# A decoder layer in one program: four cross attentions in one stretch between attention and feed-forward, and both pairs of batches through a seven-product feed-forward

## The reference

```python
def reference(x, ctx_1024, ...):            # x (4, 512, 512), ctx (4, 512, 256), float32
    ...
    x = layernorm(x + attention(x))         # 16 heads of 32, RoPE, causal softmax
    # cross attention: the context attends to itself, and its map mixes the columns of x
    query = ctx @ Wq.T + bq                 # (4, 512, 128)
    key = ctx @ Wk.T + bk
    att = softmax(query @ key.T)            # (4, 512, 512)
    x = layernorm(x + einsum('bln,bmn->blm', x, att))
    # feed-forward, hidden size 2048
    x = layernorm(x + (silu(x @ Wg.T) * (x @ Wu.T)) @ Wd.T)
```

## Time and profile before

| | |
|---|---|
| median of 3 runs | 1010.21 us (1010.11 to 1010.47) |
| profiled execution, its own time | 1012.47 us |
| its span, first to last instruction | 1010.6 us |
| granted TensorE clock, mean over the span | 0.990 |
| busy: PE, PEld, DVE, ACT, POOL | 955.7, 773.9, 690.2, 497.2, 466.3 us |
| slot 192 of the scores begins | 299.3 us |
| the first product of the pair steps begins | 755.95 us |

### The profile page before, as it was taken

The page is one execution under the profiler, slowest core; times in us unless marked ns, Lnnn a source line. Parts: engine busy times, 40 slices in busy tenths (PEclk is TensorE's granted clock), DMA queues, the critical chain, the costliest instruction groups (busy, mean ns, idle before and its releaser), DMA issues. The chain is left out here.

```text
span 1010.6 us, 15936 instructions
## 1 busy us (share of the span) xinstructions
PE 955.7 (95%) x5344; PEld 773.9 (77%) x5344; DVE 690.2 (68%) x1474; ACT 497.2 (49%) x1104; POOL 466.3 (46%) x489
## 2 busy tenths in 40 slices
PE   6788999999998889899999999999999999999997
PEld 4556877777777666688888887888887878888885
DVE  5566777778765787655555568555547888777876
ACT  4576777777775674344415433441343333332332
POOL 2466645645864523232123113212566666655644
PEclk9999999999999999899999999999999999999999
DMA  5975666955765652253212303221122121110002
GB/s 217 245 187 156 181 184 158 251 147 145 209 181 135 188 148 84 94 211 112 94 35 91 113 34 157 83 95 59 67 94 69 57 103 55 41 63 32 1 1 83
DMA packets 43040, 117.76 MB, mean 117 GB/s; under 512 B 5200, under 2 KB 5328, under 8 KB 40912
## 3 DMA queue, kind: packets, MB, share of 16 engines
q1 hardware_dynamic: 42960, 116.75, 37.7%
HBM read 91.56 MB, written 25.17 MB: 115 GB/s over the span
## 5 line engine op out<-in xcount | busy, mean ns | idle before, releaser
L961 ACT ACTIVATE prob<-prob,nmax 128x512 f32<-128x512 f32 (+3 forms) x256 | 144.0, 563 | 101.1 <-DVE nmax L1230 99.3
L1230 DVE CUSTOM_DVE_ANT_0 prob<-ps,mask 128x512 f32<-128x512 f32 (+3 forms) x256 | 124.4, 488 | 94.2 <-PE ps L649 88.7
L1672 POOL TENSOR_TENSOR g_lo<-gated,g_hi 128x512 fp32r<-128x512 f32 x32 | 41.3, 1289 | 205.5 <-ACT g_hi L1061 205.5
L649 PE MATMUL ps<-ks,qs 128*128 128x256 f32 (+2 forms) x256 | 105.1, 412 | 7.3 <-DVE nmax L1230 5.6
L1565 POOL TENSOR_TENSOR raw<-raw,cos 128x512 f32<-128x512 f32 x32 | 42.8, 1338 | 91.2 <-DVE pj L1212 64.8
L1351 DVE TENSOR_TENSOR dn_lo<-f_raw,dn_hi 128x512 fp32r<-128x512 f32 x32 | 30.5, 954 | 48.9 <-ACT dn_hi L1047 48.9
L649 PEld LDWEIGHTS ps<-ks,qs 128*128 128x128 f32 x256 | 48.9, 191 | 17.9 <-DVE nmax L1230 8.1
L634 PE MATMUL pj<-xT_hi,w_hi 128*128 128x512 f32 x128 | 52.9, 413 | 9.2 <-ACT xT_hi L931 6.1
L1574 POOL TENSOR_TENSOR raw<-raw,qk_hi 128x512 fp32r<-128x512 f32 x32 | 42.2, 1319 | 30.4 <-ACT qk_hi L955 30.4
L1374 DVE SCALAR_TENSOR_TENSOR half<-th,pg 128x512 f32<-128x512 f32 x32 | 22.0, 686 | 46.5 <-ACT th L1053 46.5
L634 PE MATMUL pj<-xT_hi,w_lo 128*128 128x512 f32 x128 | 51.4, 402 | 1.5 <-DVE w_lo L1187 1.5
(11 more groups left out here) (416 smaller groups left out, 2859.5 us busy)
## 6 DMA issues: line engine op xcount, KB each, us to landing
f_raw<-in_w_ffn SPq DMA_DIRECT2D x48, 768.0 KB, 4.2
qs<-qk_scratch SPq DMA_DIRECT2D x64, 256.0 KB, 4.6
ks<-qk_scratch SPq DMA_DIRECT2D x60, 256.0 KB, 7.4
qk_scratch<-qk_hi SPq DMA_DIRECT2D x32, 256.0 KB, 2.0
qk_scratch<-raw SPq DMA_DIRECT2D x32, 256.0 KB, 2.0
res<-in_x SPq DMA_DIRECT2D x4, 1024.0 KB, 5.8
x_scratch<-res SPq DMA_DIRECT2D x4, 1024.0 KB, 4.7
x_raw<-in_xT SPq DMA_DIRECT2D x12, 256.0 KB, 2.8
```

The source lines that it names most:

```text
L649: pe.matmul(ps[:, t % 2, 0:w], qs[n % 2][:, r, s * P:(s + 1) * P], ks[n % 2][:, r, 0:w], start=True, stop=True).then_inc(s_done, 1)
L961: act.activation(prob[:, t % PROBS, 0:w], prob[:, t % PROBS, 0:w], ACT.Exp, bias=nmax[:, n % 2, i:i + 1], scale=-1.0, accum_out=rsum[:, n ...
L1230: dve.tensor_tensor_reduce(prob[:, t % PROBS, 0:w], ps[:, t % 2, 0:w], mask[:, S - w:S], -D ** -0.5, 3e38, ALU.add, ALU.min, accum_out=nma ...
L1672: pool.tensor_tensor(g_lo[:, i % 2, :], gated[:], g_hi[:, i % 2, :].bitcast(F32), ALU.subtract).then_inc(glo_done, 1)
```

## The change

- All four cross attentions stand ahead of the feed-forward, as units in slots. That of batch 0 begins at slot 224 (table `CROSS`), those of batches 1 to 3 and the last output projections o12 to o15 are laid over one another in 45 further *ticks*, 256 to 300 (table `TICKS`; the number behind the colon is the PSUM bank, of eight). A tick is a slot without scores. Units of even and odd batches have their own sets of SBUF tiles.
- The single-batch feed-forward (`hidden`, `down`, `step`) is gone. Both pairs run through the seven products: NH = 32 pair steps. The 32 steps before had 36 matmuls each, so a pair took 72 for a hidden block; now 66.
- At the turn between the pairs (TURN = 15) the moving operands are renewed: 14 groups of four transposes (`renewed`), each with a cast on ScalarE and a remainder on VectorE, stand behind the products of step 15 and behind p1 of step 16. Step 15 has no parts, step 16 has eight. The sums for the second pair are made on GpSimd in steps 12 to 15 (`next_sums`).
- NR is 2: the load of weight block h waits for the operands of step h - 2 and for its down rows, which are now split in the step that owns them.
- The normalization after the cross attention ends on ScalarE and not on VectorE. The finished rows of batches 0 and 1 are normalized in steps 18 to 20.
- The projections q14 to k15 and o8 to o11 stand at the regular slots of every earlier group.

```diff
-ALONE = 2
-STEPS = ALONE * HT
-NR = 4
+PAIRS = B // 2
+NH = PAIRS * HT
+NR = 2
...
-BEGIN, END = -29, SCORES + 24
+BEGIN, END = -29, SCORES + 48
...
+CROSS = [(("c", 0), 224, (6,), 0), (("c", 1), 228, (6,), 0), (("t", 0), 232, (4,), 1), (("e", 0), 234, (3,), 0),
...
+         (276, "u2:5 u3:6 t8:7 t9:2"), (277, "m6:3"), (278, "e8:0 e9:1"), (279, "m7:4"), (280, "e10:0 e11:1"),
+         (281, "t10:5 t11:6"), (282, "a8:7 a9:2"), (283, "u4:5 u5:6"), (284, "a10:7 a11:2"), (285, "m8:3 u6:5"),
...
+TURN = HT - 1
+BEHIND = {(TURN, "p6"): (0, 1), (TURN, "p7"): (2, 3), (TURN, "p2"): (4, 5), (TURN, "p5"): (6, 7), (TURN, "p4"): (8, 9),
+          (TURN, "p3"): (10, 11), (TURN + 1, "p1"): (12, 13)}
...
+        def weights(h):
+
+            if h == 0:
+                full(sp, ("c", 2 * B - 1))
+            elif h == 1:
+                full(sp, ("m", 3 * ST - 1))
+            else:
+                sp.wait_ge(woplo_done, 4 * (h - 1))
+                sp.wait_ge(dnlo_done, h - 1)
...
+        def renewed(n):
+
+            name, side = SECOND_PAIR[n]
+            if n < 2:
+                pe.wait_ge(part_added, 2 * ST * (HT // 2 - 2) + ST - 1 + n)
+            else:
+                pe.wait_ge(t2lo_done, len(FIRST_PAIR) + n - 1)
+            if name[0] == "T":
+                pe.wait_ge(tnext_done, ST * {"T1": 1, "T3": 2, "T2": 3, "T4": 4}[name])
...
-        for i in range(1, STEPS):
-            hidden(i, 0)
-            hidden(i, 1)
...
-            down(i - 1)
...
-        for h in range(HT - 1):
-            product(h, "p1")
...
+        for h in range(NH - 1):
+            for name in ORDER:
+                product(h, name)
+                for n in BEHIND.get((h, name), ()):
+                    renewed(n)
...
             pair_rest(h, 0)
-            if h == 3:
-                for s in range(ST):
-                    root(1, 1, s)
-        pair_rest(HT - 1, 1)
+            if TURN - 3 <= h <= TURN:
+                next_sums(h - TURN + 3)
```

More of the change, by code:

```diff
@@ L138, with hop @@
 ENDS = {key: start + len(counts) - 1 for key, start, counts, _ in UNITS}
-def bank(b, kind, n):
-    return PLACE[kind, n][0] if b == 0 else n % 2
+CONTEXT = [unit[0] for unit in UNITS if unit[0][0] in "ceatmu"]
+def hop(key, k):
+    return ENDS[key] + HOPS[key[0]][ENDS[key] >= SCORES][k]
 def decoder_layer(nc, d, out):
@@ new lines, in program @@
+    wsum, p1 = sb("wsum", [P, 4, 2 * P]), sb("p1", [P, S])
+    wop_hi1, wop_lo1 = sb("wop_hi1", [P, 7, 2 * P], F32R), sb("wop_lo1", [P, 7, 2 * P], F32R)
+    u2, u3, th, half, gated, gated_b = (sb(n, [P, S]) for n in ("u2", "u3", "th", "half", "gated", "gated_b"))
+    f_raw.append(sb("f_raw1", [P, 2 * KT * P + E]))
+    xb = [sb(f"xb{b}", [P, ST, E]) for b in range(B - 1)]
+    with ExitStack() as third:
+        set_odd = cross_set(third, 1)
+    gates = [[sb("g_hi0", [P, 4, S], F32R), sb("g_lo0", [P, 4, S], F32R)]]
@@ L360, in full, with first_pair, second_pair @@
         eng.wait_ge(pj_full[at], index + 1)
-    def filled(eng, b, later, kind, n):
-        if b == 0:
-            full(eng, (kind, n))
-        else:
-            eng.wait_ge(later, (2 if kind == "c" else ST) * (b - 1) + n + 1)
+    def first_pair(n):
+        what, s = FIRST_PAIR[n]
+        if what == "X2":
+            return [v[:, :, s * P:(s + 1) * P] for v in x2T], KT
+        if what == "B22":
+            return [v[:, :, 2 * s * P:2 * (s + 1) * P] for v in x3T], 2
+        return [v[:, :, s // 2 * P:(s // 2 + 1) * P] for v in (t12T, t34T)[s % 2]], KT
+    def second_pair(n):
+        name, side = SECOND_PAIR[n]
+        held, k = wanted[name]
+        return [v[:, k:k + 2, 2 * side * P:2 * (side + 1) * P] for v in held]
     def emptied(eng, key):
@@ L1071, in operands @@
[L1071 to L1078 removed]
+            if b >= 2:
+                full(act, ("a", KT * (b - 1) - 1))
+            act.wait_ge(c_in[b % 2], 16 * (b // 2 + 1))
+            act.copy(c_parts[b % 2][0][:].rearrange("p k s -> p (k s)"), c_raw[b % 2][:].rearrange("p k s -> p (k s)")).then_inc(chi_done, 1)
@@ L1096, in pair_step @@
+            act.copy(pair_gated(h, b)[0], (gated, gated_b)[b][:]).then_inc(ghi_done, 1)
         def pair_step(h):
@@ L1744, in _ @@
                 residual(b)
-            if t == SPLIT_CONTEXT + 1:
-                context_rest(0)
-            for (kind, n), start, counts in CONTEXT:
-                if kind == "c" and t == ENDS[kind, n] + 3:
-                    context_query(0, n)
-                if kind == "m" and t == ENDS[kind, n] + 2:
-                    root(0, 0, n)
-            if t == FIRST_STEP:
-                step(0)
-        for i in range(1, STEPS):
-            step(i)
-        for h in range(HT):
-            if 0 < h < HT - 1:
+            for key in CONTEXT:
+                if key[0] == "c" and t == hop(key, 2):
+                    context_query(key[1])
+                if key[0] == "m" and t == hop(key, 1):
+                    root(key[1])
+            for n in range(B):
+                if t == SPLIT_CONTEXT[n] + 1:
+                    context_rest(n)
+            for s in range(ST):
+                if t == SUMS[s]:
+                    sums(s)
+            for h in range(2):
+                if t == SUM_W[h]:
+                    weight_sums(h)
+                if t == SPLIT_LOW_W[h]:
+                    operands(h)
+        for h in range(NH):
+            if 0 < h < NH - 1:
                 weight_sums(h + 1)
```

1129 lines of the change are left out of this document (489 added, 640 removed), and 18 rows, old and new, of tables (CROSS, LAST, TICKS).

## The result

The changed kernel takes 1025.8 us (median of 4 runs, 1025.0 to 1026.8) against 1010.3 us (4 runs of the kernel before): ratio 1.0148, 95% interval 1.0131 to 1.0166. It is slower by 1.5%, and the prediction, 995 us with a range of 978 to 1008, is wrong in sign. The page of the profiled execution (1025.04 us) has this at its head.

A forecast was written before the change was run, and what follows sets the result against it. The prediction took TensorE as the bound, with idle time where chains lack cover. Stages summed to 486.6 us before the first product and 509.0 after, 995.6 us; forecast 995 us, range 978 to 1008.

The forecast's parts named there:

- The count: Whole kernel, TensorE: 96 fewer matmuls, -21.8 us, and six more groups of transposes, +2.3 us; 19.5 us gained at unchanged idle time.
- Two weight buffers at nothing: Pair steps: two weight buffers in place of four cost nothing, since the block's load has 3.4 us of cover.
- The normalizations: Steps 18 to 20: eight statistics on VectorE and eight normalizations on ScalarE add 2.5 us, bounds 0 and 5.
- Nothing moves: Slots 192 to 223: projections stand as before and the cross attention is gone, so two regular groups, 43.4 us against 60.5.
- Slots 224 to 255: VectorE's work of 37.7 us and the slot order decide: 42.4 to 49 us, taken as 43.
- Ticks, 12.3 us exposed: Ticks 256 to 300: 88.6 us of TensorE work plus 4.1 us exposed in each of three cross attentions, 100.9 us.
- the chain behind e11: Ticks: maximum, exponential, small operations, scaling and four remainders take 5.0 us against 2.3 of cover, so a10 waits 2.7.
- the hand-over from a map's last transposes to the mixing: Ticks, between a11 and m8: cast, remainder and the hand-over between them expose 1.4 us.
- The turn, 41.7 us: Steps 15 and 16: 20.5 us from VectorE's work and T4's late sums, then 21.2 us of TensorE's work.
- The list of what would make it wrong: Slots from 224 taking 50 us or more, e scaling over 0.49 us, or the turn's two steps over 45 us.
- GpSimd's lock: Ticks: GpSimd holds up VectorE operations reading SBUF, ticks 140 us and kernel 1034 us if all are held; chance 0.05.
- The clock: Ticks: 30 us at 1.2 GHz would lose 15 us and leave no gain; chance of more than 13 us 0.04.

The follow-up runs named there:

- the filler: The changed kernel with 28 matmuls that nobody reads, ahead of a6, u4 and m8 in the ticks: 1021.0 us, ratio 1.0109.

## Why the prediction was wrong

By its own sum (the stages' borders are those of the prediction):

| stretch | forecast | measured |
|---|---|---|
| slots 192 to 223 | 43.4 | 48.5 |
| slots 224 to 255 | 43.0 | 46.9 |
| ticks | 100.9 | 112.6 |
| pair steps 0 to 14 | 218.8 | 218.0 |
| turn, step 15 | 20.5 | 24.9 |
| turn, step 16 | 21.2 | 28.1 |
| steps 17 to the end | 248.5 | 244.0 |
| span (with 299.3 and 300.2 to slot 192) | 995.6 | 1023.3 |

**The count** was right: 72 instructions fewer, and pair steps full. **Two weight buffers at nothing** was right: TensorE never waits for f_raw (GpSimd does, 30 times and for 84.1 us in all, off the path), and the steps take 14.97 us, shorter than the 15.21 forecast. The normalizations, forecast at 2.5 us, show as 1.2 us in step 20. The last stretch is shorter than forecast by 4.5 us for these two reasons.

**"Nothing moves" in slots 192 to 223** failed. The cross attention went, but its context split stayed in front of a rotation in GpSimd's queue. Before, the same split showed as the wait of 3.0 us for c_lo; the step took it for a part of what goes away. It measured 4.7 us (48.5 to 43.8 when the split was moved).

**Slots 224 to 255** lie within the bounds given, 42.4 to 49 us. VectorE is busy for 37.12 of 46.9 us, 0.79 and near the sparser of the two rows; I took the denser one. No run here varies this stage.

**Ticks, 12.3 us exposed.** The idle time, 13.2 us, was nearly that size, and yet the mechanism was wrong. Its step says that TensorE is the longer, by totals of 88.6 against 78 us, and that what counts is the chain behind e11. The totals hide that VectorE's work is bunched: cutting the chain, turning the queues and both left the idle time (13.8, 13.2 and 13.3 us between the last slot and the first product, against 14.1); moving mixings into the dense stretch made the ticks 6 us shorter. One part of the chain did measure as priced: the hand-over from a map's last transposes to the mixing, 1.4 us in the forecast, was 1.45 us ahead of m8. What was missing in the sum is, first, the clock, 4.5 us, which the step kept "within the bounds" at nothing. The 39 groups of transposes started every 0.435 us and not every 0.38 (the earlier trace rows has 0.80 for two groups, so 0.40 was the reading), which is 2.1 us. With 0.9 us more idle time that is 7.5 of the 11.7 us missed; the rest is not accounted for.

**The turn, 41.7 us.** For step 15 the forecast counted VectorE's work, 17.1 us behind a start at 2.7, and T4's sums done at 18 us, 20.5 us for the step. With both orders turned the step took 20.0 us, so as load that was right. What it missed is the order: VectorE's remainders stood behind the sum of a product that TensorE makes only after the next transposes, which makes the two engines take turns. T4's sums, behind the gated rows, were done only 23.6 us into the step, and the step took 24.9. The section on the change shows this very order, and the prediction reads it as load. Step 16 missed by more: "TensorE's: 90 matmuls and two groups, 21.2" has no wait in it, and it took 28.1. Of that, 3.2 us are idle time, 2.1 of them the wait for a part that VectorE adds behind the sum of p4, and 3.1 us are the clock (6.1 us at 1.2 GHz). Even without renewals the step took 23.2 us. The list of what would make it wrong had the turn over 45 us, and that is what happened.

**The rivals.** The slower one, GpSimd's lock, is not what happened. The scaling of e:

```profile
L1214 DVE TENSOR_SCALAR e<-e,erec x16: 485/486/1085, 370.8 to 492.6; 128x512 f32<-128x512 f32 x16
```

its median is what it was, 486 ns against a mean of 488. Three of 16 took longer, 1085, 755 and 589 ns (at 378.9, 461.7 and 461.0 us), and these are the three that ran beside one of GpSimd's sums of 128x256 or more for most of their time; together they lost 1.0 us. The Trainium skill (SBUF — State Buffer, Who interferes with whom) says that such an operation can contend with GpSimd for the port; the trace agrees for those three. The clock was given 0.04 for over 13 us lost in the ticks, which had 10.2 us at 1.2 GHz, some 5 us lost. Over the whole span the granted clock took 0.023 x 1023.3 - 0.010 x 1010.6 = 13.4 us more than before, but 8.5 of them lie ahead of slot 192, which begins only 0.9 us later. From slot 192 to the last stretch there are 23.9 us at 1.2 GHz in place of 13.7, 5.1 us lost. They came with the idle time, as the filler shows, and were no rival of their own. The Trainium skill (TensorE: Matmul & The Clock Gate, What's actually happening) has activity as what lifts the clock, and the run with the filler agrees.

What stays open: the turn's last 12 us over the version without renewals (46.2 against 33.9, of which some 6 are transposes), the stage of slots 224 to 255, and how much of the ticks' idle time is VectorE's load and how much the order on ScalarE.
